# Cellular automaton: its two f32 products as three passes of rounded high and low parts

## The reference

```
h       = relu(conv3x3(x, Wp) + bp)        # 8 -> 32 channels, same padding
nca_out = sigmoid(conv1x1(h, Wu) + bu)     # 32 -> 8 channels
```

## Time and profile before

| what | value |
|---|---|
| median of three runs | 3454.14 us |
| the profiled execution, its own time | 3450.26 us |
| its span, first to last instruction | 3448.4 us |
| mean granted TensorE clock | 0.922 |
| stage `nca`, first load issued to last sigmoid ended | 537.2 to 723.8 us |

### The profile page before, as it was taken

How to read it: one execution, slowest core, us unless ns; L and a number is a source line. 1 busy time by engine, 2 the same in 40 slices (tenths; PEclk the granted TensorE clock), 3 DMA queues, 4 the chain that set the end, 5 groups by cost and what they waited for, 6 DMA issues and landing times. The chain is left out here.

```text
span 3448.4 us, 44291 instructions
## 1 busy us (share of the span) xinstructions
PE 2794.9 (81%) x16948; PEld 2101.2 (61%) x16948; DVE 1863.9 (54%) x2412; ACT 1404.4 (41%) x2331; POOL 705.8 (20%) x653
## 2 busy tenths in 40 slices
PE   0699997969666199569996799769996699999658
PEld 0344441126344199569995799669995687887535
DVE  6888773327534411254554445354454578878643
ACT  1877773422122122153333333253333466666322
POOL 3988500012110000000000000000000044444310
PEclk9999998989788599889998999979998899999879
DMA  8200005569424455958767677657776624332134
GB/s 212 60 24 0 24 17 142 155 154 198 126 89 143 89 130 134 219 157 190 194 156 205 146 184 195 164 164 178 182 189 176 126 52 91 56 61 51 62 89 94
DMA packets 344104, 437.92 MB, mean 127 GB/s; under 512 B 260535, under 2 KB 302135, under 8 KB 317519
## 3 DMA queue, kind: packets, MB, share of 16 engines
q1 hardware_dynamic: 343428, 430.41, 51.8%
q0 software_dynamic: 496, 5.01, 0.4%
HBM read 258.59 MB, written 168.58 MB: 124 GB/s over the span
## 5 line engine op out<-in xcount | busy, mean ns | idle before, releaser
L1026 DVE STREAM_TRANSPOSE spec_chan<-spec_form_in 128x1024 f32<-128x1024 f32 x256 | 492.1, 1946 | 62.2 <-PE fno_pz L1242 62.2
L1328 ACT ACTIVATE fno_act<-fno_pz 128x320 f32<-128x320 f32 x512 | 224.0, 437 | 616.1 <-PE fno_pz L1242 616.1
L1412 DVE COPY fno_wfreq<-fno_pw 128x240 f32<-128x240 f32 x256 | 97.8, 395 | 513.7 <-PE fno_pw L1270 511.8
L1217 POOL TENSOR_SCALAR fno_minus<-fno_both 96x960 f32<-96x960 f32 x32 | 83.4, 2607 | 1376.8 <-DVE fno_both L1420 1376.8
L1242 PEld LDWEIGHTS fno_pz<-spec_cols,spec_chan 128*128 128x128 f32 x3072 | 348.2, 192 | 12.3 <-issue 9.5
L1242 PE MATMUL fno_pz<-spec_cols,spec_chan 128*128 128x96 f32 x3072 | 350.0, 275 | 2.0 <-ACT spec_cols L1336 2.0
L1293 PE MATMUL fno_pz<-fno_act,fno_wt 128*40 128x64 f32 x2304 | 204.5, 263 | 149.5 <-DMA fno_act<-scratch_modes 107.1
L1270 PE MATMUL fno_pw<-fno_fw,fno_act 128*128 128x96 f32 x2560 | 303.4, 277 | 14.4 <-DVE fno_wfreq L1412 8.6
L1546 POOL TENSOR_TENSOR head_hact_lo<-head_hact,head_hact_hi 128x512 fp32r<-128x512 f32 x128 | 227.9, 1783 | 400.4 <-DVE head_hact_hi L1693 400.4
L1270 PEld LDWEIGHTS fno_pw<-fno_fw,fno_act 128*128 128x128 f32 x2560 | 291.4, 192 | 26.9 <-DVE fno_wfreq L1412 15.4
L1293 PEld LDWEIGHTS fno_pz<-fno_act,fno_wt 128*40 128x40 f32 x2304 | 197.6, 139 | 158.8 <-issue 146.0
(11 more groups left out here) (158 smaller groups left out, 4628.4 us busy)
## 6 DMA issues: line engine op xcount, KB each, us to landing
scratch_form<-fno_act SPq DMA_DIRECT2D x32, 2560.0 KB, 17.2
spec_form_in<-scratch_form SPq DMA_DIRECT2D x64, 1024.0 KB
fno_act<-scratch_modes SPq DMA_DIRECT2D x128, 180.0 KB
nca_win<-scratch_xnp SPq DMA_DIRECT2D x66, 329.7 KB
fno_coef<-scratch_mixed SPq DMA_DIRECT2D x48, 360.0 KB, 10.8
spec_form_in<-scratch_form SPq DMA_DIRECT2D x32, 512.0 KB
fno_wt<-table_mix_w SPq DMA_DIRECT2D x32, 450.0 KB, 11.1
gn_x<-scratch_x SPq DMA_DIRECT2D x12, 1024.0 KB
```

What stands on the lines that cost most here:

```text
L1026: return nc.vector.transpose(chan[:, to * TR * PIX:(to + 1) * TR * PIX].rearrange("p (h q w) -> p h q w", h=TR, q=4), src)
L1328: nc.scalar.activation(act_b[:, n % 2, :, 4 * t:4 * t + 4], z, ACT.Silu if layer else ACT.Copy).then_inc(a_out, 1)
```

## The change

Only `nca` and its tables change. The bias bp becomes a 121st row of the weight matrix, against a 121st row of ones in the window, which one DMA writes once. The window's tile is now called `raw` and has 3 slots. GpSimd copies each window into `win_hi` (fp32r, rounded), VectorE writes `win_lo` = raw - win_hi. VectorE does the same once for the two weight matrices. Each product becomes three fp32r passes into one bank. The hidden layer's high part, relu(conv) rounded, comes from ScalarE (`hid_hi`), the low part, max(conv, 0) - hid_hi, from VectorE (`hid_lo`), each with 4 slots. TensorE's point products stand two quarters behind the conv instead of one; ScalarE does relu(n), then sigmoid(n-3). SyncE loads window v+3 once VectorE has read slot v. The `Fori` loops are gone: all 88 quarters are written out, with waits on constants.

```diff
-    K, MH, MO = 3 * (R1 + 2) * C, R1 * HID, R1 * C
+    K, MH, MO = 3 * (R1 + 2) * C + 1, R1 * HID, R1 * C
+    SLOTS, RING = 3, 4
...
+                sp.dma_start(raw[K - 1:K, :, 0:ROWP - 2], k["nca_one"]).then_inc(tables, 16)
+                load(0)
+                for dst, src in ((wmat, "nca_w"), (wumat, "nca_u"), (buc, "nca_bu")):
                     sp.dma_start(dst[:, :], k[src]).then_inc(tables, 16)
-                load(R1, 1)
-                with sp.Fori(0, WIN1 // 2 - 1) as i:
-                    for s in range(2):
-                        sp.wait_ge(conv_done, i * QW + (s + 1) * NQ)
-                        load(i * 2 * R1 + (s + 2) * R1, s)
-                        store(i, s)
+                load(1)
+                load(2)
+                for v in range(WIN1):
+                    if v + SLOTS < WIN1:
+                        sp.wait_ge(split_lo, v + 1)
+                        load(v + SLOTS)
+                    sp.wait_ge(out_ready, (v + 1) * NQ)
+                    sp.dma_start(ncp[v * R1 + 1:v * R1 + 1 + R1].rearrange("h c f -> (h c) f"), out[:, v % 2, :]).then_inc(stored[v % 2], 16)
...
+            @block.gpsimd
+            def _(pool):
+                for v in range(WIN1):
+                    if v == 0:
+                        pool.wait_ge(tables, 64)
+                    pool.wait_ge(loaded[v % SLOTS], 48 * (v // SLOTS + 1))
+                    if v >= SLOTS:
+                        pool.wait_ge(conv_done, (v - SLOTS + 1) * NQ)
+                    nc.gpsimd.tensor_copy(win_hi[:, v % SLOTS, 0:ROWP - 2], raw[:, v % SLOTS, 0:ROWP - 2]).then_inc(split_hi, 1)
...
+                def low_part(v):
+                    x, o, hi = (t[:, v % SLOTS, 0:ROWP - 2] for t in (raw, win_lo, win_hi))
+                    dve.wait_ge(split_hi, v + 1)
+                    nc.vector.tensor_tensor(o, x, hi.bitcast(F32), ALU.subtract).then_inc(split_lo, 1)
+                low_part(0)
+                for n in range(N):
+                    if n % NQ == 1 and n // NQ + 1 < WIN1:
+                        low_part(n // NQ + 1)
+                    dve.wait_ge(hi_ready, n + 1)
+                    nc.vector.scalar_tensor_tensor(out=hid_lo[:, n % RING, :], in0=conv[:, n % 4, :], scalar=0.0, in1=hid_hi[:, n % RING, :].bitcast(F32),
+                                                   op0=ALU.max, op1=ALU.subtract).then_inc(lo_ready, 1)
...
+                def point_of(n):
+                    pe.wait_ge(lo_ready, n + 1)
+                    if n >= 4:
+                        pe.wait_ge(out_ready, n - 3)
+                    for part, (w, x) in enumerate(((wumat_hi, hid_hi), (wumat_hi, hid_lo), (wumat_lo, hid_hi))):
+                        mm = nc.tensor.matmul(point[:, n % 4, :], w[:, :], x[:, n % RING, :], start=part == 0, stop=part == 2)
+                    mm.then_inc(point_done, 1)
+                for n in range(N):
+                    s, q = n // NQ % SLOTS, n % NQ
+                    if q == 0:
+                        pe.wait_ge(split_lo, n // NQ + 1)
+                    if n >= 4:
+                        pe.wait_ge(lo_ready, n - 3)
+                    for part, (w, x) in enumerate(((wmat_hi, win_hi), (wmat_hi, win_lo), (wmat_lo, win_hi))):
...
+                    if n >= 2:
+                        point_of(n - 2)
...
+                for n in range(N):
+                    act.wait_ge(conv_done, n + 1)
+                    if n >= RING:
+                        act.wait_ge(point_done, n - RING + 1)
+                    nc.scalar.activation(hid_hi[:, n % RING, :], conv[:, n % 4, :], ACT.Relu).then_inc(hi_ready, 1)
+                    if n >= 3:
+                        sigmoid_of(n - 3)
```

More of the change, by code:

```diff
@@ L162, in laid_out @@
     c["nca_u"] = m.reshape(R1 * HID, R1 * C)
[L163 removed]
+    c["nca_bu"] = col(inp["L0_conv_bu"], R1)
     m = z(R2 + 2, C, 3, 3, R2, C)
@@ L596, in nca @@
         point = ph.ps("point", [MO, 4, NB])
[L597 to L600, removed]
+        tables, zeroed, weights = ph.sem("tables"), ph.sem("zeroed"), ph.sem("weights")
+        loaded, stored = [ph.sem(f"loaded{s}") for s in range(SLOTS)], [ph.sem("stored0"), ph.sem("stored1")]
+        split_hi, split_lo, conv_done, hi_ready, lo_ready, point_done, out_ready, border = (
+            ph.sem(n) for n in ("split_hi", "split_lo", "conv_done", "hi_ready", "lo_ready", "point_done", "out_ready", "border"))
+        N = WIN1 * NQ
         with nc.Block() as block:
@@ L635, in _ @@
             @block.vector
             def _(dve):
-                open_at_one(dve, hid_ready)
                 nc.vector.memset(zero[:, :], 0.0).then_inc(zeroed, 1)
                 nc.vector.memset(out[:, :, :], 0.0).then_inc(zeroed, 1)
-                dve.wait_ge(tables, 16 * 4)
-                with dve.Fori(0, WIN1 // 2) as i:
-                    for n in range(QW):
-                        dve.wait_ge(conv_done, i * QW + n + 1)
-                        dve.wait_ge(point_done, 1 + i * QW + max(0, n - 1))
-                        nc.vector.tensor_scalar(hid[:, n % 2, :], conv[:, n % 4, :], bpc[:, :], 0.0, ALU.add, ALU.max).then_inc(hid_ready, 1)
+                dve.wait_ge(tables, 64)
@@ L649, in _ @@
             def _(pe):
[L650 to L669 removed]
+                pe.wait_ge(weights, 4)
@@ L671, in _ @@
+                point_of(N - 2)
+                point_of(N - 1)
             @block.scalar
             def _(act):
-                open_at_one(act, out_ready)
                 act.wait_ge(zeroed, 2)
-                act.wait_ge(tables, 16 * 4)
-                with act.Fori(0, WIN1 // 2) as i:
-                    for n in range(QW):
-                        act.wait_ge(point_done, 1 + i * QW + n + 1)
-                        s, q = n // NQ, n % NQ
-                        if q == 0:
-                            act.wait_ge(stored[s], 1 + i * 16)
-                        o = out[:, s, :].rearrange("p (b w) -> p b w", b=B)[:, q * BPB:(q + 1) * BPB, 1:W + 1]
-                        nc.scalar.activation(o, point[:, n % 4, :].rearrange("p (b w) -> p b w", w=W), ACT.Sigmoid, bias=buc[:, :]).then_inc(out_ready, 1)
+                act.wait_ge(tables, 64)
@@ new lines, in sigmoid_of @@
+                def sigmoid_of(n):
+                    act.wait_ge(point_done, n + 1)
+                    v, q = n // NQ, n % NQ
+                    if q == 0 and v >= 2:
+                        act.wait_ge(stored[v % 2], 16 * (v // 2))
+                    o = out[:, v % 2, :].rearrange("p (b w) -> p b w", b=B)[:, q * BPB:(q + 1) * BPB, 1:W + 1]
+                    nc.scalar.activation(o, point[:, n % 4, :].rearrange("p (b w) -> p b w", w=W), ACT.Sigmoid, bias=buc[:, :]).then_inc(out_ready, 1)
@@ L687, in gate @@
+                for n in range(N):
[5 more added lines that the diff above has]
+                        sigmoid_of(n - 3)
+                for n in range(N - 3, N):
+                    sigmoid_of(n)
 def gate(nc, k, xnp, cmp_, ncp, x0, x1):
```

59 lines of the change are left out of this document (24 added, 35 removed).

## The result

The changed kernel takes 3425.48 us in the median of seven runs (3419.07 to 3440.48), the kernel before 3454.84 us (3449.07 to 3459.65). The ratio is 0.9925, with 95% confidence between 0.9907 and 0.9943 (the quotient of the two medians is 0.9915): faster, by somewhat more than forecast. The profiled execution took 3424.0 us with a span of 3422.0.

A forecast was written before the change was run, and what follows sets the result against it. The prediction took TensorE as the bound: 3450.26 - 21.5 for shorter work + 5.0 for the later start = 3433.8 us, with the median's offset 3437. Its own range was 3430 to 3444, for 8 in 10 3428 to 3462.

The forecast's parts named there:

- the likeliest case: The forecast with its small variants, for the whole kernel: range 3430 to 3444 us, chance 0.58.
- The cost of a turn: TensorE's surplus where conv and point shapes alternate, 0.17 and 0.11 us per quarter, expected to stay in the new kernel.
- Rival (d): Turns between shapes cost nothing once the list is written out; window 6.3 to 6.5 us; 3430 us; chance 0.08.
- The chain of the loads: SyncE's load behind the store, then copy, low part, subtraction: in time for TensorE, slack 0.25 us.
- The copy: GpSimd's rounding copy of each 121 x 2110 window from f32 to fp32r takes 2.4 us.
- Rival (a): GpSimd's copy takes 5.7 us, adding 1.0 us per window and 3.3 at the start; 3463 us, chance 0.14.
- (b): Copy about 4 us, or loads slower by as much under the shorter period; 3449 us or no tellable change; chance 0.15.
- The collision of (a): VectorE's low part, with two SBUF inputs, waits out GpSimd's copy of the next window if the copy exceeds some 4 us.
- ScalarE: Relu 0.69 us and sigmoid 0.68, with waits 1.47 of a 1.69 us quarter, hidden behind TensorE.
- (c): ScalarE loads its table at each turn between relu and sigmoid, 225 us in all; 3660 us, chance 0.03.
- The start: First product 5.0 us later, since the first conv waits for window, copy, 2.35 us low part and 0.2 of waits.
- Clock: TensorE's first 5.3 us of work run at the lower 1.2 GHz level, adding 2.6 us.

The follow-up runs named there:

- e1: Kernel before with the point product's 24 columns zero-padded to 96, still f32 and in loops; 3438.51 us, ratio 0.9956.
- e3: Kernel after with the point product as one f32 product of the high part instead of three fp32r passes; 3451.09 us, ratio 0.9996.
- e4: Kernel after with each store one window later in SyncE's order, behind the next load; 3420.43 us, ratio 0.9914.
- e11: e4 with VectorE's low part of each window computed in two halves; 3412.81 us, ratio 0.9875.
- e5: Kernel after with GpSimd copying each window twice, first into a spare tile nobody reads; 3456.84 us, ratio 1.0006.
- e6: e4 with each window loaded by one DMA of 120 partitions instead of three of 40; 3581.61 us, ratio 1.0363.
- e9: e1 with loops written out and one load DMA per window instead of three; 3581.88 us, ratio 1.0371.
- e12: e11 with the tables and the row of ones issued on ScalarE's queue instead of SyncE's; 3423.71 us, ratio 0.9906.

## Why the prediction was nearly right, step by step

The direction and the mechanism of the forecast held: TensorE's shorter passes bring the gain, and part goes back through the start and the chain of the loads. 3425.5 us lies 11.5 below 3437, below the likeliest case's own range (3430 to 3444), and 2.5 below the lower end of the wide one (3428 to 3462); as a ratio it stands just at that end, 0.9925 against 3428 / 3454.14 = 0.9924. Two steps were mis-sized, in opposite directions, so that the number is as near as it is is partly luck.

- **The cost of a turn, "and it stays in the new kernel".** This failed. It was booked at 0.28 us per quarter, 24.6 us for 88, and is nothing. (Nor were the turns of before 88: 77 pairs of them, see e1, so that its 88 quarters took 173.9 us and not 176.) The quarter was put at 1.69 and is 1.41. e1 and e3 show from both sides that an f32 product of 24 columns beside a wide one makes the turn. Nothing in the trace of before told fp32r from f32 here, since neither the gate nor the spectral operator alternates shapes in the rows that I took; I should have held it as open with both ends, 1.41 and 1.69. Rival (d) had the size and the wrong cause.
- **The chain of the loads.** It was put at a slack of 0.25 us, so at no stall, with 2 us for uneven loads; it costs 0.9 us per window, 16.8 in all. The links were right: copy 1.95 us (2.4 forecast), low part 2.354 (2.35), subtraction 0.681 (0.69 to 0.75). Two were too short. From the load's issue to the copy's start it takes 8.6 us in the mean (8.2 to 9.7), where 0.9 + 6.6 = 7.5 was forecast, and SyncE needs 0.36 us from the last sigmoid's end to the load's issue, because it issues the store first. So from that sigmoid's end to the start of the point that waits for the chain it is 14.0 us, where the prediction has 13.3. More weighs what the shorter quarter does: nine quarters lie between the release and the need, so 0.28 us off each takes 2.5 us off the time allowed, which was 13.5 us by the forecast and is 11.3. 14.0 - 11.3 = 2.7 us, over three windows 0.9 each, and 0.9 is what the window shows. e4 shows the chain by cutting it (9.8 us of stage back, window 5.87). The forecast for (d), 6.3 to 6.5 us per window, came within 0.04 to 0.24 of it.
- **The copy.** Rival (a), and (b) as far as it speaks of the copy, are refuted by 1.948 us; (b)'s other half, loads slower under the shorter period, holds in part, with 1.1 us of its 1.6 (8.6 against 7.5). The estimate of 1.8 us from the Trainium skill ("GPSIMD Engine Reference", on elementwise cost) was nearer than mine. The collision of (a) is real (e4's 4.62 us), and there almost harmless; in after the two never meet in steady course, as forecast.
- **ScalarE.** 0.594 + 0.665 us of 1.41, no table load between relu and sigmoid in 176 activations: (c) is refuted. The Trainium skill, "ScalarE: Activation LUTs", "Table sets: the hidden batching unit", had relu in every set; the trace now agrees.
- **The start.** +5.5 us against +5.0. "The weights' small operations fall under the copy" held not quite: VectorE's cast of 96 x 24 took 1.91 us, the copy's length, and the two subtractions stand between copy and low part, 0.34 us in all.
- **Clock.** 0.65 in the first 5 us of work, full from 559 on; no more than forecast.

The sum with the measured sizes: the 88 quarters take 173.9 - 124.1 = 49.8 us less; the stalls cost 16.8 (21 of them), the slow first passes and the end of the list 0.5 more than before, the start 5.5: 27.0, against 26.9 measured for the stage. Against the forecast of 155.7 us for the work, which took 144.6: 24.6 less for the turns, 14.8 more for stalls (16.8 against 2), 1.3 less for the slow passes and the end.

Behind the sum, the offset of 3.9 us between the profiled execution and the median came out smaller: 3425.48 to 3424.0 is 1.5. Two slips in the prediction's figures change nothing: 1.60 us is 20% below 2.00 and not 18, and the chances that it names as faster add up to 0.70 and not 0.68.

## What to carry to other kernels

Before splitting an f32 product, look at the distance between products of different shapes: if a narrow one stands beside a wide one, padding the narrow one's columns takes the turn away at once. When a bound engine gets faster by a third, work the loads' chain out again with the new period and with the whole time from the load's issue to the start of the work that it releases in it, and keep a store that waits for late results from standing ahead of a load that doesn't need them. If a link of that chain is long and in one piece on a busy engine, cut it in two: in e11 the wait behind it fell from 10.9 to 2.8 us.

## What the runs showed of the hardware that was not expected

- An f32 product of 24 columns alternating with one of 96: 2.00 us per pair, of 64 columns 2.03; of 96 with 96: 1.73. Six fp32r passes, 24 columns beside 96: 1.41, no extra.
- A VectorE cast with a single SBUF input, 96 x 24, took 1.91 us beside GpSimd's copy, so one input is not enough to be safe. The Trainium skill, "SBUF — State Buffer", "Who interferes with whom", adds what the prediction had left out: a cast can enter a mode with two ports and then contends. The subtraction with one input in PSUM never did (681 ns in the mean).
- A stall of 4.0 us in an otherwise full stretch (e5) was followed by some 5.5 us with passes 0.42 us apart, at a granted clock of 0.50 to 0.54. After's stalls, up to 1.8 us between two passes once a window, left the clock at 1.00.
- A load with an outermost dimension of 3 had three packets under way at a time and took 13.4 us per window (e6, e9); three loads of 40 partitions had ten, and the window's traffic fits into 5.66 us (e12).
